# Second channel block's convolution moved from VectorE to TensorE in a gated-convolution stage, with the stage's written-out order redone

## The chip, the cores and the metric

The kernel runs on one core of a Trainium2 chip. The metric is the device time of one execution in microseconds (us). Three timed runs stand for the kernel before, and one further execution was profiled. Engines are called PE (TensorE matmul; its weight loads are listed apart as PEld), DVE (VectorE), ACT (ScalarE), POOL (GpSimd) and SP (SyncE).

## The reference

Two pre-norm layers over x of shape (8, 512, 256), float32 throughout: a selective-scan block, an attention block with a four-expert mixture, a gated-convolution block, and a second mixture. The change touches only the third, which the kernel calls stage D. Its core is:

```
xz = layernorm(x) @ W_in                       # (8,512,256) @ (256,1024)
xc, z = split(xz, 2)                           # 512 channels each
xc = causal depthwise conv, 4 taps, over the 512 positions
xc = layernorm(silu(xc), gamma, beta)
xp = xc @ W_xproj                              # 33 columns: delta, B(16), C(16)
delta = clip(softplus(xp[..., :1]))
decay = clip(exp(delta * A), 1e-6, 1)          # per position, channel and state (16)
y = xc * sum_n(B*C * decay) + xc * D
x = x + (y * silu(z)) @ W_out
```

## The kernel before, in words

The kernel is five stages, A to E, run one after the other; all five engines meet between stages. In stage D the 8 sequences are the 8 batches. The 512 channels are four blocks of 128 (c = 0 to 3, one block across the partitions), and the 512 positions are the free dimension.

**Preparing a batch.** `stats`, `rstd`, `minus` and `norm` are the layernorm; `flip` (PE, L1964) transposes it and `flipped` (ACT, L2062) evacuates it. `lift` (PE, L1974) makes one of 8 blocks of the input projection: 0 to 3 are the convolution's channels, 4 to 7 the gate z. `lifted` (ACT, L2062) evacuates it. The convolution of a block is done in one of two ways. `conv` (PE, L1982) does it as four accumulating 128x512 matmuls with a diagonal matrix for each tap, and `conved` (ACT, L2062) evacuates the result; `taps` (DVE, L2185 and L2188) does it as one tensor_scalar and three scalar_tensor_tensor. Before the change, block 0 goes through `conv` and blocks 1, 2 and 3 through `taps`. `silu` (ACT) loads an activation table, takes silu of the convolved channels (L2100), then of z (L2103), and loads the exponential's table again (L2104). `turnx` (PE, L1989) transposes 16 tiles, `stats2` (DVE, the lines L192 and L196 on PSUM), `rstd2` and `xn` (L2201) are the second layernorm, `back` (PE, L1997) transposes back, `xf` evacuates with gamma and beta, `xproj` (PE, L2006) is the 33-column projection. `pj`, `soft`, `clip`, `rep` (PE, L2015) and `scalars` (DVE, L2225 and L2227) spread delta and B*C over the partitions. `fetch` and `add` (DVE, L2167) complete the next batch's x from gathered rows.

**The units.** A batch is also 16 units; over all batches unit u runs from 0 to 127, and 4 units in turn make a group w. `grow(u)` (ACT, L2131) is an exponential over 128x2048, `scale(u)` (DVE, L2237) is four tensor_scalar that clip it and multiply by B*C, in place, in one of 10 buffers. `sum(w, q)` (PE, L2024; q = 0 to 3) sums the four units of a group over the states; q = 0 waits for `scale(4w+3)`. `wout` (ACT, L2137) evacuates the sums, `turnw` (PE, L2034) transposes them, `gate` (DVE, L2247) adds D and multiplies by silu(z)*xc, `proj` (PE, L2042) is the output projection and `acc` (DVE, L2253) adds to x.

**The order** is written out by hand, and each engine walks its own share of one list in order. At list position u the list holds `grow(u+2)`, `scale(u)`, one `sum(w, q)` with 4w+4+q = u, the steps of END at their distance from 4w+4, and one row of the plan of each batch in work. A batch x > 0 takes its plan, PLAN, one row a position, so that row k stands at position u = 16(x-1) - 10 + k; 24 rows make it overlap the plan of the next batch by 8 rows. Batch 0 takes START, which begins at position -26. PSUM products of the plan rotate through 4 banks; a product waits for the evacuation of the one four before it. The rule that sets how far ACT can run ahead is `grow(4w+10)`, which waits for `sum(w, 3)`.

These are the rows of PLAN and END that matter here, as they are before:

```
(("flipped", 0), ("flipped", 1), ("lift", 1)), (("lifted", 1), ("lift", 2)), (("taps", 1), ("lifted", 2)),
(("lift", 3),), (("lifted", 3), ("taps", 2), ("lift", 0)), (("lifted", 0), ("lift", 4)),
(("taps", 3), ("lifted", 4), ("conv", 0)), (("conved", 0), ("lift", 5)),
(("lifted", 5), ("lift", 6), ("lift", 7)), (("lifted", 6), ("lifted", 7)), (("silu",),),
END = ((4, "wout"), (5, "turnw"), (7, "gate"), (8, "proj"), (9, "acc"))
```

The first of these is row 4 of PLAN, the one with `silu` is row 14, `turnx` is row 15, `stats2` is row 16 together with the next batch's `stats` (its row 0), `xn` 17 and 18, `back` 19, `xf` and `xproj` 20, `rep` 22.

Of the kernel before, what the change touches and what calls it, by code (L numbers as in the profile page):

```python
# [25 lines left out]
class Arena:  # L26
    def __init__(self, tensor, start, end):
        self.t, self.at, self.end = tensor, start, end
# [186 lines left out]
def take_stats(ar):  # L215
    return ar.take([4, 6]), ar.take([4, 2]), ar.take([4])


class StageA:
# [89 lines left out]
    def over(self, *step):  # L309
# [29 lines left out]
        (23, ("stepped", 3), ("softh", 1), ("cliph", 1), ("duh", 1), ("fill", 0, 1), ("drive", 0, 1)), (24, ("lifted", 1), ("lifted", 2), ("lifted", 3)))  # L339
    END = (  # L340
        (3, ("recall",)), (4, ("odd",)), (8, ("back", 0)), (9, ("gate", 0), ("back", 1)),
        (10, ("gate", 1), ("back", 2), ("gate", 2), ("back", 3)), (12, ("gate", 3), ("proj", 0, 0), ("proj", 0, 1)),
        (13, ("proj", 0, 2), ("proj", 0, 3), ("proj", 0, 4)), (14, ("proj", 0, 5), ("proj", 0, 6), ("proj", 0, 7)),
        (16, ("back_to_x", 0), ("proj", 1, 0)), (17, ("proj", 1, 1), ("proj", 1, 2)),
        (18, ("proj", 1, 3), ("proj", 1, 4), ("proj", 1, 5), ("proj", 1, 6), ("proj", 1, 7)), (20, ("back_to_x", 1)))
# [3 lines left out]
    def order(self):  # L349
# [3 lines left out]
        for h in range(first - 32, 2 * K + 32):  # L353
            b, j = divmod(h, 32)
            k, f = divmod(h, 2)
            if h == self.FIRST - 32:
                out += [("tap", w) for w in range(4)] + [("tapped", w) for w in range(4)]
            pieces = [(what, y, *rest) for y in range(NB - 1) for at, *steps in self.END if at == h - 32 * (y + 1)
                      for what, *rest in steps]
# [1476 lines left out]
class StageD:  # L1836
# [6 lines left out]
    def __init__(self, m, c):  # L1843
        self.m, self.c = m, c
        ar = Arena(m.Z, m.LO, m.HI)
        self.gy = [ar.take([256]) for _ in range(4)]
        self.An = ar.take([4, 512])
        self.wout = ar.take([4, 256])
        self.win = ar.take([2, 1024])
        self.wxp = ar.take([4, 33])  # L1850
        self.rep = ar.take([4, 128])
        self.pick = ar.take([32])
        self.diag = ar.take([4, 128])
        self.dcol = ar.take([4])
        self.sb, self.sb2 = take_stats(ar), take_stats(ar)
        self.nb = ar.take([4])
        self.pj = ar.take([4, 33])
        self.src = ar.take([4, 17])
        self.dl = [ar.take([4, 4]) for _ in range(2)]
        self.bc = [ar.take([16, 4]) for _ in range(2)]  # L1860
        self.nf = ar.take([2, 512])
        self.xp = ar.take([4, 515])
        self.nt = ar.take([4, 256])
        self.xc = ar.take([4, 512])
        self.z = ar.take([4, 512])
        self.xn, self.xf = self.xp[:, :, 3:515], self.xc
        self.zx = [ar.take([4, 512]) for _ in range(2)]
        self.e = [ar.take([4, 512]) for _ in range(10)]
        self.wt = [ar.take([512]) for _ in range(2)]
        self.yf = [ar.take([4, 128]) for _ in range(2)]  # L1870
        self.wb, self.tb, self.ob = m.banks[0:2], m.banks[2], m.banks[3]
        self.steps = self.order()
        self.uses = {}
        for step in self.steps:
            if step[0] in ("flip", "lift", "conv", "turnx", "back", "xproj", "rep"):
                self.uses[step] = len(self.uses)
        self.ring = m.ring(m.banks[4:8], len(self.uses))
        self.d_gy = m.landings(0, 4, 32)
        self.s = {n: m.sem("d_" + n) for n in (
            "d_w", "d_a", "added", "pads", "an", "consts", "moments", "rstd", "nb", "nt", "prod", "conv", "gate", "xc",  # L1880
            "xn", "bc", "raw", "dl", "sc", "zx", "grow", "scale", "sum", "wt", "tw", "yf", "op", "acc")}

    def use(self, *step):
# [2 lines left out]

    PLAN = (
        (("stats",),), (("rstd",), ("minus",)), (("norm",),), (("flip", 0), ("flip", 1)),
        (("flipped", 0), ("flipped", 1), ("lift", 1)), (("lifted", 1), ("lift", 2)), (("taps", 1), ("lifted", 2)),
        (("lift", 3),), (("lifted", 3), ("taps", 2), ("lift", 0)), (("lifted", 0), ("lift", 4)),  # L1890
        (("taps", 3), ("lifted", 4), ("conv", 0)), (("conved", 0), ("lift", 5)),
        (("lifted", 5), ("lift", 6), ("lift", 7)), (("lifted", 6), ("lifted", 7)), (("silu",),),
        (("turnx", 0), ("turnx", 1), ("turnx", 2), ("turnx", 3)), (("stats2",),), (("rstd2",), ("xn", 3)),
        (("xn", 0), ("xn", 1), ("xn", 2)), (("back", 0), ("back", 1), ("back", 2), ("back", 3)),
        (("xf", 0), ("xf", 1), ("xf", 2), ("xf", 3), ("xproj",)), (("zx",), ("pj",), ("soft",)),
# [2 lines left out]

    START = (
        (("stats",), ("consts",)), (("rstd",), ("minus",), ("spread",)), (("norm",), ("decay",)), (("flip", 0), ("flip", 1)),  # L1900
        (("flipped", 0), ("flipped", 1), ("lift", 1)), (("lifted", 1), ("lift", 2)),
        (("lifted", 2), ("taps", 1), ("lift", 3)), (("lifted", 3), ("taps", 2), ("lift", 0)),
        (("lifted", 0), ("conv", 0)), (("conved", 0), ("taps", 3), ("lift", 4)), (("lifted", 4), ("lift", 5)), (("lifted", 5), ("lift", 6)),
        (("lifted", 6), ("lift", 7)), (("lifted", 7), ("silu",), ("bound",)),
        (("turnx", 0), ("turnx", 1), ("turnx", 2), ("turnx", 3)), (("stats2",),), (("rstd2",),),
        (("xn", 0), ("xn", 1), ("xn", 2), ("xn", 3)), (("back", 0), ("back", 1), ("back", 2), ("back", 3)),
        (("xf", 0), ("xf", 1), ("xf", 2), ("xf", 3), ("xproj",)), (("pj",), ("zx",), ("soft",)),
        (("clip",), ("rep",)), (("scalars",),))


    END = ((4, "wout"), (5, "turnw"), (7, "gate"), (8, "proj"), (9, "acc"))

    def order(self):
        N, out = 16 * NB, []
        for u in range(-27, N + 12):
# [6 lines left out]
            if w in range(N // 4):  # L1922
                out.append(("sum", w, j))
            for at, what in self.END:
                y = u - 4 - at
# [26 lines left out]
    def pe(self, e):  # L1952
        m, s, ring, ident = self.m, self.s, self.ring, self.m.ident
        def bank(*step):
            r = self.use(*step)
            if r >= 4:
                e.wait_ge(*ring.done(r - 4))
            return ring.buf(r)
# [18 lines left out]
        def conv(b, c):  # L1977
            e.wait_ge(s["consts"], 1)
            e.wait_ge(*ring.done(self.use("lift", b, c)))
            o = bank("conv", b, c)  # L1980
            for w in range(4):
                ins = e.matmul(o, self.diag[:, w, :], self.xp[:, c, w:w + 512], start=w == 0, stop=w == 3)  # L1982
            ins.then_inc(s["prod"], 1)

        def turnx(b, i):
# [51 lines left out]
        def proj(w):  # L2037
# [3 lines left out]
            for k in range(4):  # L2041
                ins = e.matmul(self.ob[:, 0:256], self.yf[w % 2][:, k, :], self.wout[:, k, :], start=k == 0, stop=k == 3)  # L2042
            ins.then_inc(s["op"], 1)

        self.walk(flip=flip, lift=lift, conv=conv, turnx=turnx, back=back, xproj=xproj, rep=rep, sum=sums, turnw=turnw,
                  proj=proj)

    def act(self, e):
        m, s, ring, own, vec = self.m, self.s, self.ring, self.m.own["act"], self.m.vec
# [45 lines left out]
            evac(self.xc[:, c, :], "conv", b, c)  # L2095

        def silu(b):
            e.wait_ge(*ring.done(self.use("conv", b, 0)))
            e.wait_ge(s["conv"], 3 * b + 3)
            e.activation(self.xc, self.xc, ACT.Silu).then_inc(s["xc"], 1)  # L2100
            for c in range(4, 8):
                e.wait_ge(*ring.done(self.use("lift", b, c)))
            e.activation(self.z, self.z, ACT.Silu).then_inc(s["gate"], 1)  # L2103
            e.preload_act_table_set(LN_EXP)  # L2104
# [28 lines left out]
        def wout(w):  # L2133
            e.wait_ge(s["sum"], w + 1)
            if w >= 2:
                e.wait_ge(s["tw"], w - 1)
            e.activation(self.wt[w % 2], self.wb[w % 2], ACT.Copy).then_inc(s["wt"], 1)  # L2137

        self.walk(decay=decay, rstd=rstd, norm=norm, flipped=flipped, lifted=lifted, conved=conved, silu=silu, rstd2=rstd2, xf=xf,
                  soft=soft, grow=grow, wout=wout)  # L2140

    def dve(self, e):
        m, s, ring, own, vec = self.m, self.s, self.ring, self.m.own["dve"], self.m.vec
        def consts(b):
            e.wait_ge(s["pads"], 1)
            for w in range(4):
                e.tensor_scalar(self.diag[:, w, :], m.ident, vec["conv1"][:, w:w + 1], None, ALU.mult)

        def spread(b):
            for j in range(4):  # L2150
# [100 lines left out]
        def acc(w):  # L2251
            e.wait_ge(s["op"], w + 1)
            e.tensor_tensor(m.X[:, w, :], m.X[:, w, :], self.ob[:, 0:256], ALU.add).then_inc(s["acc"], 1)  # L2253

        self.walk(consts=consts, spread=spread, bound=bound, add=add, stats=stats, minus=minus, taps=taps, stats2=stats2, xn=xn, pj=pj, clip=clip, scalars=scalars,
                  scale=scale, gate=gate, acc=acc)

# [438 lines left out]
```

## Time and profile before

| | |
|---|---|
| timed runs (3) | median 3223.49 us, 3222.7 to 3224.59 |
| profiled execution | 3224.59 us, its span 3222.8 us |
| stage D in the trace | about 2104 to 2674 us |
| mean granted TensorE clock | 0.936 of full speed |
| busy over the whole span | PE 86%, DVE 66%, ACT 50%, POOL 32% |

The stage is a sixth of the span. A row of the timeline gives the start, the time taken, the engine, the line, the shapes and, in brackets, how long the engine had been idle before it and what ended that. The profile records two matmul instructions for each float32 matmul of the code, so a `conv` of four matmuls is "x8".

### The profile page before, as it was taken

How to read it: one execution, taken by the hardware profiler on the slowest of the kernel's cores; microseconds unless marked ns; L12 is line 12 of the kernel's file. 1: busy time of each engine (PE TensorE's matmuls, PEld its weight loads, DVE VectorE, ACT ScalarE, POOL GpSimd, SP SyncE). 2: the span in 40 equal slices, each digit the busy share in tenths (PEclk: the TensorE clock that was granted, in tenths of full speed). 3: DMA queues.
4: the chain of work that ended last, by engine and by line, in shares of the span. 5: the costliest groups of instructions: out<-in, count | busy, mean ns of one | idle time of the engine just before them, and what ended most of it. 6: DMA issues, size and time to landing. Idle time of an engine off the chain costs nothing.

```text
span 3222.8 us, 40373 instructions
## 1 busy us (share of the span) xinstructions
PE 2765.5 (86%) x13718; PEld 1663.7 (52%) x13718; DVE 2132.6 (66%) x3858; ACT 1623.9 (50%) x2429; POOL 1021.4 (32%) x714
## 2 busy tenths in 40 slices
PE   7778887887765799999969999958888988999999
PEld 4445454454443455555545666634444445666666
DVE  1788888888885667777532222237777785777776
ACT  3778778877861355555441111137787781111111
POOL 0788888888881221121001000011112000100000
PEclk9899999999867899999989999978989999999999
DMA  3587887888873665555422000020000002000000
GB/s 112 120 175 148 173 174 163 148 181 169 161 176 80 191 175 95 88 93 79 68 118 80 23 23 23 15 53 11 7 7 14 1 1 59 7 14 7 7 7 14
DMA packets 119273, 262.95 MB, mean 82 GB/s; under 512 B 14784, under 2 KB 72896, under 8 KB 117408
## 3 DMA queue, kind: packets, MB, share of 16 engines
q0 software_dynamic: 24928, 134.89, 20.1%
q1 hardware_dynamic: 94144, 125.47, 16.9%
q8 instruction: 115, 1.88, 0.3%
q14 instruction: 86, 0.70, 0.1%
HBM read 135.40 MB, written 131.20 MB: 83 GB/s over the span
## 4 chain that ended last, share of the span: by engine, by line
PE 49%; issue 7%; ACT 6%; DVE 5%; DMA 1%; POOL 0%; POOLq 0%; ACTq 0%; DVEq 0%
PE PS L2401 7%; PE PS L1677 6%; PE PS L2419 6%; PE PS L1974 4%; PE PS L1699 3%; PE PS L1340 2%; ACT Z L2131 2%; PE PS L2024 2%; PE PS L1297 2%; PE PS L1319 2%; PE PS L1322 2%; PE PS L1267 2%; PE PS L2006 1%; PE PS L1272 1%; PE PS L1366 1%
## 5 line engine op out<-in xcount | busy, mean ns | idle before, releaser
L856 POOL TENSOR_TENSOR Z<-Z 128x1024 f32<-128x1024 f32 x256 | 649.4, 2764 | 123.1 <-DVE Z L757 77.4
L764 DVE TENSOR_TENSOR_SCAN Z<-PS,Z 128x1024 f32<-128x1024 f32 x256 | 576.4, 2275 | 19.6 <-ACT PS L684 10.8
L535 PE MATMUL PS<-Z 128*128 128x128 f32 x2048 | 305.4, 295 | 120.9 <-DVE Z L764 48.4
L535 PEld LDWEIGHTS PS<-Z 128*128 128x128 f32 x2048 | 250.5, 151 | 253.0 <-issue 80.1
L684 ACT ACTIVATE PS<-Z 128x511 f32<-128x511 f32 x512 | 332.7, 687 | 65.2 <-DVE Z L764 63.4
L1436 ACT ACTIVATE Z<-PS 128x512 f32<-128x512 f32 x320 | 188.9, 596 | 269.0 <-PE PS L1322 263.8
L2452 ACT ACTIVATE Z<-PS 128x512 f32<-128x512 f32 x144 | 85.9, 596 | 411.8 <-PE PS L2401 411.8
L696 ACT ACTIVATE Z<-PS,Z 128x512 f32<-128x512 f32 x378 | 245.6, 683 | 75.9 <-PE PS L535 69.3
L2401 PE MATMUL PS<-Z 128*128 128x512 f32 x576 | 273.5, 600 | 7.9 <-DVE Z L2534 7.1
L1529 DVE TENSOR_REDUCE Z<-PS 128x1 f32<-128x512 f32 (+2 forms) x384 | 182.5, 507 | 122.1 <-PE PS L1298 118.4
L2131 ACT ACTIVATE Z<-Z 128x2048 f32<-128x2048 f32 x128 | 252.6, 1999 | 14.5 <-PE PS L2024 8.8
L487 PE MATMUL PS<-Z 128*128 128x512 f32 x512 | 243.3, 604 | 10.3 <-ACT Z L604 9.5
L1677 PE MATMUL PS<-Z 128*128 x560 | 247.8, 595 | 0.6 <-issue 0.6
L2419 PE MATMUL PS<-Z 128*128 128x256 f32 x1024 | 242.9, 380 | 2.1 <-DVE Z L2549 2.1
L2419 PEld LDWEIGHTS PS<-Z 128*128 128x128 f32 x1024 | 193.6, 190 | 80.6 <-issue 53.6
L2237 DVE TENSOR_SCALAR Z<-Z 128x512 f32<-128x512 f32 x512 | 215.3, 488 | 7.5 <-ACT Z L2131 7.2
L2549 DVE SCALAR_TENSOR_TENSOR Z<-PS,Z 128x256 f32<-128x256 f32 x512 | 213.7, 475 | 9.9 <-PE PS L2419 9.9
L2534 DVE TENSOR_TENSOR Z<-Z,PS 128x512 f32<-128x512 f32 x144 | 98.2, 686 | 131.0 <-ACT Z L2452 130.6
L1804 DVE TENSOR_TENSOR Z<-Z,PS 128x512 f32<-128x512 f32 x70 | 48.1, 687 | 197.2 <-PE PS L1677 197.2
L2278 POOL TENSOR_TENSOR Z<-Z 128x512 f32<-128x512 f32 x32 | 41.5, 1327 | 428.5 <-ACT Z L2062 428.5
L2024 PE MATMUL PS<-Z 128*32 128x512 f32 x1024 | 142.0, 645 | 35.3 <-DVE Z L2237 35.3
L1677 PEld LDWEIGHTS PS<-Z 128*128 128x128 f32 x560 | 104.3, 191 | 119.2 <-issue 119.2
(297 smaller groups left out, 4930.2 us busy)
## 6 DMA issues: line engine op xcount, KB each, us to landing
sums<-Z POOLq DMA_DIRECT2D x112, 768.0 KB, 8.5
Z<-rows_b SPq DMA_DIRECT2D x128, 256.0 KB, 4.8
Z<-scr SPq DMA_DIRECT2D x256, 128.0 KB, 6.9
rows_n<-in_L_ffn_expert_wv POOLq DMA_DIRECT2D x32, 528.0 KB, 7.8
scr<-Z SPq DMA_DIRECT2D x32, 384.0 KB, 3.5
Z<-Z POOLq DMA_DIRECT2D x14, 768.0 KB, 7.5
Z<-in_L_ffn_expert_wv SPq DMA_DIRECT2D x4, 2048.0 KB, 15.1
Z<-sums SPq DMA_DIRECT2D x7, 768.0 KB, 6.3
```

The costliest lines, as they stand in the source:

```text
L487: ins = e.matmul(self.bank("conv", b, c)[0], self.conv[:, w, k, c * 128:(c + 1) * 128], self.n_fm[:, k, w:w + 512], start=i == 0, stop=i == 7)
L535: ins = e.transpose(self.turned[i % 2][:, c * 128:(c + 1) * 128], self.h(k, c // 2)[:, c % 2, i * 128:(i + 1) * 128], ident)
L684: ins = e.activation(self.aa[f][:, c, 1:512], self.de[b % 2][:, 2 * f + c, 1:512], ACT.Exp, scale=self.An[:, q:q + 1])
L696: e.activation(self.pr[k % 3][:, i - 1, :], self.turned[i % 2], ACT.Copy, scale=self.ct[b % 2][:, i, 16 + n:17 + n]).then_inc(s["yprod"], 1)
L764: e.tensor_tensor_scan(h, a, h, 0.0, ALU.mult, ALU.add).then_inc(s["scan"], 1)
L856: e.tensor_tensor(self.h(k, f), self.du[b % 2][:, 2 * f:2 * f + 2, :], b3(self.Bs[k % 2], 1, [128, 2, 512]), ALU.mult).then_inc(s["hin"], 1)
L1677: ins = e.matmul(ub[n], self.hs[c % 2][:, k, :], self.wv[:, bass.ds(expert[c] * 4096 + (2048 * k + 512 * n), 512)], start=k == 0, stop=k == 1)
L2131: e.activation(self.e[u % 10], self.An, ACT.Exp, scale=self.dl[b % 2][:, j, i:i + 1]).then_inc(s["grow"], 1)
L2237: ins = e.tensor_scalar(o, o, 1e-6, self.bc[b % 2][:, 4 * j + i, q:q + 1], ALU.max, ALU.mult)
L2401: ins = e.matmul(self.up[n % 2], w, self.nf[b % 2][:, k, :], start=k == 0, stop=k == 1)
L2419: ins = e.matmul(o[:, j * 256:(j + 1) * 256], self.hd[n % 4][:, c], self.w2[:, x - 1, :], start=True, stop=True)
L2549: ins = e.scalar_tensor_tensor(xx, o[:, j * 256:(j + 1) * 256], self.cw[b % 2][:, t, x - 1:x], xx, ALU.mult, ALU.add)
```

## The change

Block 1's convolution goes to PE as well. The diagonal matrices are built for blocks 0 and 1 (8 instead of 4 tensor_scalar at the start of the stage), `conv(1)` and `conved(1)` come into both plans and `taps(1)` goes out. The rows 4 to 14 of PLAN and the rows from 4 on of START are written anew: the lifts come in the order 2, 3, 0, 1, 4, 5, 6, 7, and `lift` 5, 6, 7 now stand together in row 13 with `lifted` 6, 7 in the row of `silu`. Row 15 on are as before, but START is two rows longer, so that `turnx` to `scalars` of batch 0 come two positions later against the plan of batch 1. In END `wout` moves from 4 to 3, `proj` from 8 to 9 and `acc` from 9 to 11.

```diff
-        self.diag = ar.take([4, 128])
+        self.diag = ar.take([2, 4, 128])
...
     PLAN = (
...
-        (("flipped", 0), ("flipped", 1), ("lift", 1)), (("lifted", 1), ("lift", 2)), (("taps", 1), ("lifted", 2)),
-        (("lift", 3),), (("lifted", 3), ("taps", 2), ("lift", 0)), (("lifted", 0), ("lift", 4)),
-        (("taps", 3), ("lifted", 4), ("conv", 0)), (("conved", 0), ("lift", 5)),
-        (("lifted", 5), ("lift", 6), ("lift", 7)), (("lifted", 6), ("lifted", 7)), (("silu",),),
+        (("flipped", 0), ("flipped", 1), ("lift", 2)), (("lifted", 2), ("lift", 3)), (("taps", 2), ("lift", 0)),
+        (("lifted", 3), ("lifted", 0), ("taps", 3), ("lift", 1)), (("lifted", 1), ("conv", 0)),
+        (("conved", 0), ("conv", 1)), (("lift", 4), ("conved", 1)), (), (("lifted", 4),),
+        (("lift", 5), ("lifted", 5), ("lift", 6), ("lift", 7)), (("lifted", 6), ("lifted", 7), ("silu",)),
...
     START = (
...
-        (("flipped", 0), ("flipped", 1), ("lift", 1)), (("lifted", 1), ("lift", 2)),
-        (("lifted", 2), ("taps", 1), ("lift", 3)), (("lifted", 3), ("taps", 2), ("lift", 0)),
-        (("lifted", 0), ("conv", 0)), (("conved", 0), ("taps", 3), ("lift", 4)), (("lifted", 4), ("lift", 5)), (("lifted", 5), ("lift", 6)),
-        (("lifted", 6), ("lift", 7)), (("lifted", 7), ("silu",), ("bound",)),
+        (("flipped", 0), ("flipped", 1), ("lift", 2)), (("lifted", 2), ("lift", 3)),
+        (("lifted", 3), ("taps", 2), ("lift", 0)), (("lifted", 0), ("taps", 3), ("lift", 1)), (("bound",),),
+        (("lifted", 1), ("conv", 0)), (("conved", 0), ("conv", 1))) + (
+        (("conved", 1), ("lift", 4)), (("lifted", 4), ("lift", 5)), (("lifted", 5), ("lift", 6)),
+        (("lifted", 6), ("lift", 7)), (("lifted", 7), ("silu",)),
...
-    END = ((4, "wout"), (5, "turnw"), (7, "gate"), (8, "proj"), (9, "acc"))
+    END = ((3, "wout"), (5, "turnw"), (7, "gate"), (9, "proj"), (11, "acc"))
...
-                ins = e.matmul(o, self.diag[:, w, :], self.xp[:, c, w:w + 512], start=w == 0, stop=w == 3)
+                ins = e.matmul(o, self.diag[:, c, w, :], self.xp[:, c, w:w + 512], start=w == 0, stop=w == 3)
...
         def silu(b):
-            e.wait_ge(*ring.done(self.use("conv", b, 0)))
-            e.wait_ge(s["conv"], 3 * b + 3)
+            for c in range(2):
+                e.wait_ge(*ring.done(self.use("conv", b, c)))
+            e.wait_ge(s["conv"], 2 * b + 2)
...
-            for w in range(4):
-                e.tensor_scalar(self.diag[:, w, :], m.ident, vec["conv1"][:, w:w + 1], None, ALU.mult)
+            for c in range(2):
+                for w in range(4):
+                    e.tensor_scalar(self.diag[:, c, w, :], m.ident, vec["conv1"][:, 4 * c + w:4 * c + w + 1], None, ALU.mult)
```

## Rows read from the trace of the kernel before

**Rows 1.** Window in stage D: length; busy PE, PEld, DVE, ACT, POOL; clock; DMA; GB/s.

```profile
2310.00:2370.00 60.00, 52.72 (x268) 25.63 (x268) 45.25 (x118) 48.09 (x47) 9.32 (x8) 0.91 0.03 10
```

**Rows 2.** Who waited for whom, 2186 to 2661 us: total, times, longest.

```profile
DVE Z L2253 <- PE PS L2042: 29.7, 12, 4.1
...
PE PS L2024 <- DVE Z L2237: 34.0, 11, 4.5
...
PE PS L1989 <- ACT Z L2100: 13.5, 7, 4.4
...
PE PS L1964 <- ACT Z L2062: 8.8, 6, 2.4
```

**Rows 3.** Timeline of PE, 2250 to 2300 us (batch 2).

```profile
2252.48 3.60 PE L1982 MATMUL PS<-Z 128*128 128x512 f32 x8
2256.01 1.06 PE L2024 MATMUL PS<-Z 128*32 128x512 f32 x8
...
2260.31 3.70 PE L1974 MATMUL PS<-Z 128*128 128x512 f32 x8
2263.94 1.92 PE L2024 MATMUL PS<-Z 128*32 128x512 f32 x16
...
2270.90 1.97 PE L1989 MATMUL PS<-Z 128*128 128x128 f32 x16 [1.52 <-ACT Z L2100]
...
2279.22 1.93 PE L2024 MATMUL PS<-Z 128*32 128x512 f32 x8 [4.50 <-DVE Z L2237]
```

**Rows 4.** Timeline of PE, the same `turnx` one batch on.

```profile
2335.91 1.97 PE L1989 MATMUL PS<-Z 128*128 128x128 f32 x16 [1.52 <-ACT Z L2100]
```

**Rows 5.** Groups by line, 2186 to 2661 us: busy us, mean ns.

```profile
L2188 DVE SCALAR_TENSOR_TENSOR Z<-Z 128x512 f32<-128x512 f32 x62 | 46.6, 752 | 2.2
...
L2185 DVE TENSOR_SCALAR Z<-Z 128x512 f32<-128x512 f32 x20 | 9.7, 485 | 10.6 <-ACT Z L2062 10.6
```

**Rows 6.** Timeline of ACT, 2262 to 2285 us.

```profile
2267.04 0.58 ACT L2137 ACTIVATE Z<-PS 128x512 f32<-128x512 f32 x1
2267.64 1.28 ACT L2100 ACT_TABLE_LOAD   x1
2268.93 1.91 ACT L2100 ACTIVATE Z<-Z 128x2048 f32<-128x2048 f32 x1
```

**Rows 7.** Timeline of DVE, 2262 to 2283 us.

```profile
2273.00 2.49 DVE L192 BATCH_NORM_STATS2 Z<-PS 128x6 f32<-128x512 f32 x4 [1.83 <-PE PS L1989]
...
2275.82 1.37 DVE L192 BATCH_NORM_STATS2 Z<-Z 128x6 f32<-128x256 f32 x4
...
2277.52 1.64 DVE L2237 TENSOR_SCALAR Z<-Z 128x512 f32<-128x512 f32 x4
```

**Rows 8.** Granted clock in two stretches of batch 2 (columns as in rows 1).

```profile
2278.00:2286.00 8.00, 6.78 (x24) 2.94 (x24) 8.00 (x20) 7.94 (x12) 0.00 (x0) 0.57 0.00 0
2295.00:2299.00 4.00, 4.00 (x13) 1.46 (x16) 2.18 (x7) 0.51 (x2) 3.09 (x4) 0.57 0.23 66
```

**Rows 9.** Timeline of PE, 2115 to 2206 us (batch 0 and the start).

```profile
2137.23 3.67 PE L1982 MATMUL PS<-Z 128*128 128x512 f32 x8 [0.73 <-issue]
...
2164.24 3.65 PE L1997 MATMUL PS<-Z 128*128 128x128 f32 x16 [9.32 <-DVE Z L2201]
2169.08 7.01 PE L2006 MATMUL PS<-Z 128*128 128x33 f32 x32 [1.19 <-ACT Z L2062]
...
2178.58 3.75 PE L1974 MATMUL PS<-Z 128*128 128x512 f32 x4 [0.73 <-issue]
```

**Rows 10.** Timeline of DVE, the start of the stage.

```profile
2119.15 0.84 DVE L2147 TENSOR_SCALAR Z<-Z 128x128 f32<-128x128 f32 x4
...
2157.88 1.40 DVE L2167 TENSOR_TENSOR Z<-Z 128x256 f32<-128x256 f32 x4
```

**Rows 11.** Timeline of ACT, first `grow` and batch 1's `silu`.

```profile
2185.86 2.00 ACT L2131 ACTIVATE Z<-Z 128x2048 f32<-128x2048 f32 x1
...
2202.62 1.28 ACT L2100 ACT_TABLE_LOAD   x1
```

## The prediction

> **What bounds the stage now.** I read four views, in this order: the busy times of a steady stretch, the list of waits, the timeline of each engine over one batch, and the granted clock of short windows.
>
> The steady stretch [rows 1] shows PE busy 52.72 of 60 us, ACT 48.09 and DVE 45.25. One batch takes 2335.91 - 2270.90 = 65.0 us, from `turnx` to the next `turnx` [rows 3, 4]. PE idles only three times in it. It waits 1.52 us for `silu` ahead of `turnx` and 4.50 us for `scale` behind it [rows 3], and some 1.3 us for `xf` (8.8 us in 6 times, the last wait of [rows 2]). So PE works 65.0 - 7.3 = 57.7 us of a batch. DVE has its own idle time, 29.7 us in all at `acc` [rows 2], and PE doesn't wait for what comes behind those. Hence in a steady batch the sum of PE's work and of its three waits is the time. A microsecond put on PE costs one, a microsecond taken from DVE gives nothing, unless it shortens one of the waits.
>
> That PE is really occupied while it is recorded as busy can be read from starts alone: `conv` starts at 2252.48 and the next matmul at 2256.01, 3.53 us for 8 instructions of 512 columns, 0.44 us each, with nothing between [rows 3].
>
> The Trainium skill, Perfetto Trace Analysis, Identifying the Most-Contended Engine, says that matmul busy time is no measure of PE's headroom and that LDWEIGHTS busy share is one, while for VectorE and ScalarE occupancy is a fair measure. By it PE (PEld 25.63 of 60) would have room, and ACT and DVE would be the contended engines. I go by the spacing of the starts, but the rule's outcome is a rival below.
>
> **The change in a steady batch (batches 2 to 7).**
>
> - *Added on PE: `conv(1)`.* 3.53 us at full clock [rows 3]. Bounds: the fall of a clock to half would make it 7.1; below 3.53 nothing in the trace suggests.
> - *Removed from DVE: `taps(1)`.* 0.485 + 3 x 0.752 = 2.74 us [rows 5]. DVE idles in each batch anyway, so 0 on the path.
> - *Added on ACT: `conved(1)`*, in place of nothing; the like evacuation is 0.58 us (`wout`, [rows 6]). ACT is idle for the whole of `conv` now, so 0.
> - *`wout` one position earlier.* It then waits for the same `sum(w, 3)` as the `grow` behind it, which it delays by 0.58 us; that `grow` is followed by the same work in sum. 0.
> - *`proj` and `acc` later.* PE's order changes (`proj` behind `sum` 1 and `turnw` instead of behind `sum` 0), its sum doesn't. The wait of `acc` for `proj`, 29.7 us of DVE, should all but go, since two positions lie between them now. Behind it on DVE stood the next batch's `add` and a `scale` which no PE wait hangs on. 0.
> - *The wait ahead of `turnx`.* It ends with `silu`, so I compare both ways from t, the start of `lift(5)` behind `sum` 3 in row 13. PE: three lifts at 3.63 / 2 (2260.31 to 2263.94) are 5.4 us. From 2263.94 to the end of `turnw` at 2270.90 - 1.52 = 2269.38 PE now does three sums, `proj` and `turnw` in 5.44 us; one of the sums (0.96, half of the 1.92) is ahead of t in the new order. So PE is at `turnx` at t + 5.4 + 4.5 = t + 9.9. ACT: `lift(7)` ends at t + 5.4, then 0.1 of latency, `lifted(7)` 0.6, table load 1.28, `silu` 1.91 [rows 6]: t + 9.3. PE comes second, the wait goes: -1.52. The margin is 0.6 us.
> - *The wait of 4.50 us behind `turnx`.* `turnx` starts at 2270.90; DVE can begin `stats2` at 2273.00, was idle for 1.83 us before it, and then runs `stats2`, the next batch's `stats` and `scale` (2277.52 + 1.64) without a gap [rows 7]. PE has two sums to do meanwhile. Every instruction of this chain and its order stay (rows 15 to 18 of the plan are untouched). `acc` now falls behind this `scale`, not in front. 4.50 us stay.
> - *Clock.* After that wait the granted clock is at half for (1 - 0.57) x 2 x 8 = 6.9 us, and again behind `xproj` for 3.4 us of a window of 4 [rows 8]. PE is idle for 0.6 us of the first, so the two cost it about 3.1 + 1.7 = 4.8 us in a batch. What stands ahead of each (4.50 us of idle time; `xproj` with its 33 columns) stays, and I take the same 4.8. The bounds are 1.7 (one short fall) and 6.8 (two long ones).
>
> The sum is 3.53 - 1.52 = +2.0 us a batch, six times +12.1. The bounds from the clock alone are 6 x (-3.1) = -19 and 6 x 2.0 = +12 around it.
>
> The Trainium skill, TensorE: Matmul & The Clock Gate, The HAM clock gate, has the clock fall after an idle stretch and come back after a busy one; the falls of this trace agree, one behind 4.50 us of idle time [rows 3, 8]. It gives no reason why a fall should go here, as the stretch of 4.50 stays.
>
> **The start of the stage and batch 1.** PE isn't the bound in it, so I follow the chain.
>
> - Four more diagonals on DVE stand between `stats` and `minus`: +0.84 [rows 10].
> - `conv(1)` of batch 0: +3.53; the 0.73 us that PE waited ahead of `conv(0)` [rows 9] goes, as `lift(1)` now lies between: together +2.8.
> - The `add` and `stats` of batch 1 stood between `stats2` and `xn` of batch 0. In the new order they come ahead of `stats2`, where DVE has nothing to do: -1.40 [rows 10] - 1.70 (2275.82 to 2277.52, [rows 7]), but the second layernorm's two small activations, hidden behind them so far, come out: +0.5. Together -2.6.
> - `flip` of batch 1 now stands ahead of `back(0)` on PE. Eight transposes are half of 3.65, 1.8 us [rows 9], half of it beside `xn`: +0.9.
> - `lift(2)` of batch 1 stands ahead of `xproj(0)`: 3.6 us at half clock (3.75 for the row at 2178.58) less the 1.19 that PE waits there now [rows 9]: +2.4.
> - From the end of `xproj` (2176.09) to the first `grow` (2185.86) lie 9.8 us [rows 9, 11]. `flip` and the gap up to 2178.58 leave it: -2.5.
> - From that `grow` to batch 1's table load are 16.8 us [rows 11], ACT without a break. ACT will have to wait for the two convolutions in it: `conv(0)` ends about 4.9 us and `conv(1)` 8.4 us after the first `grow` starts, ACT is there 0.7 and 1.1 us before: +1.8.
>
> These make +0.84 + 2.8 - 2.6 + 0.9 + 2.4 - 2.5 + 1.8 = +3.6, if the clock stays at half up to the second lift. `xproj(0)` takes 7.01 us at half clock [rows 9]; PE is busy for longer ahead of it than now, and at full clock it and a lift would save 3.5 + 1.8, which makes it -1.7. The upper bound is another lift at half clock, +5.4. I take the middle, +2.
>
> **The end of the stage.** The last batch has no successor to prepare and keeps its chain; of `proj(30)` and `turnw(31)` the order is swapped. Between -0.6 and 0; I take 0.
>
> **Sum.** 12.1 + 2.0 = +14.1 us on the profiled execution's 3224.59 (its span 3222.8), that is 3238.7. It stands 1.1 us above the median of the runs, so the predicted median is 3237.6, +0.44%. This kernel's measurement can tell about 0.2%, 6.4 us.
>
> **Rivals.**
>
> 1. *The clock falls become rarer (no measurable change).* The time that PE idles around `turnx` shrinks from 6.0 to 4.5 us, and the batch's length changes, so the falls will lie elsewhere. For it speaks that the falls follow idle time. Against it speaks that the 4.50 us stay. If each batch loses the long fall's 3.1 us or the short one's 1.7, that is 14.1 - 19 = -5 or 14.1 - 10 = +4 us: 3219 to 3228. If both go, 14.1 - 29 = -15: 3209.
> 2. *PE has room and DVE sets the pace (faster).* PE's recorded 52.72 of 60 would be partly pipelining, `conv(1)` would slip in at no cost, and DVE's 2.74 us a batch would come off: 6 x -2.74 + 2 = -14 us, 3209. It decides from the point where the matmul behind `conv(1)` starts less than 0.8 us later than without it. Against it speaks the unbroken spacing [rows 3]. It is what the skill's rule on the most-contended engine leads to.
> 3. *The wait behind `turnx` shrinks (faster).* Its place is `sum` 0 in row 18; DVE has 2.74 us less in a batch and no wait at `acc`. It decides from 2.4 us on, since then 2.0 a batch and the start are paid; all 4.50 us would make 6 x (2.0 - 4.5) + 2 = -13 us, 3210. Against it speaks that DVE was idle ahead of `stats2` [rows 7].
> 4. *The wait ahead of `turnx` stays (slower still).* The lifts 5 to 7 and `silu` stand closer together now and the margin is 0.6 us. If ACT is late by as much as now, it is 6 x 1.52 = 9 us more: 3247.
>
> **How the numbers follow.** The forecast, 3230 to 3244, has 0.52. Rival 1 has 0.17 for the part within 0.2% and 0.02 for both falls gone, rivals 2 and 3 have 0.06 and 0.04, rival 4 0.12; 0.07 is left for a new wait on PE that I don't see, slower too. Faster by over 0.2% is 0.02 + 0.06 + 0.04 = 0.12, within it 0.17, slower 0.52 + 0.12 + 0.07 = 0.71. The range leaves out the faster rivals (0.12), the lower end of rival 1 and the far end of the slower cases (0.08): 3226 to 3246.
>
> **What the profile after would show.** L1982 with 128 instructions, L2188 with 48; a batch of 67 us from `turnx` to `turnx`; the wait of L1989 for L2100 near 0 from batch 2 on; the waits of PE's L2024 for L2237 still 4.5 us each; DVE's wait of L2253 for L2042 nearly gone; batch 1's table load 2 us later than now. I am wrong if the 4.50 us shrink, if half-clock time in a batch changes by over 3 us, or if PE shows a new wait at `conv`, `rep` or `turnx`.

## The result, and the profile after

The kernel after took 3249.3 us in the median of 4 runs (3245.37 to 3251.26), the kernel before 3224.04 us (4 runs, 3222.7 to 3227.59): a ratio of 1.0076, 95% interval 1.0057 to 1.0093. Slower was forecast, but 3237.6 us with at most 3246. In the third set of experiments below the same two kernels stood at 1.0051 (1.0033 to 1.007), 3246.53 against 3229.94 us. The loss is clear of the noise both times, and its size varies.

The profiled execution of the kernel after took 3246.3 us, its span is 3244.5 us, 21.7 more than before. Windows cut both spans at the start of stage D, at the `turnx` of batch 1, at that of batch 7 and at the end of stage D. The kernel before (columns as in [rows 1]):

```profile
2103.80:2205.88 102.08, 60.03 (x185) 34.15 (x185) 46.90 (x116) 48.80 (x59) 16.51 (x17) 0.73 0.16 42
2205.88:2597.76 391.88, 347.14 (x1769) 166.12 (x1769) 296.18 (x765) 306.48 (x295) 51.40 (x44) 0.91 0.03 8
2597.76:2673.96 76.20, 63.17 (x416) 30.95 (x416) 63.98 (x165) 58.13 (x43) 5.66 (x4) 0.96 0.00 1
2673.96:3222.80 548.84, 527.16 (x1920) 350.22 (x1920) 388.28 (x937) 99.69 (x185) 48.65 (x80) 0.99 0.06 17
```

The kernel after:

```profile
2104.08:2202.62 98.54, 61.68 (x200) 33.80 (x200) 42.77 (x112) 50.55 (x61) 16.92 (x17) 0.77 0.16 44
2202.62:2614.42 411.80, 372.40 (x1817) 180.52 (x1817) 280.63 (x740) 306.47 (x301) 52.17 (x44) 0.90 0.02 7
2614.42:2690.88 76.46, 62.40 (x417) 32.22 (x416) 60.74 (x166) 58.09 (x43) 7.63 (x4) 0.93 0.00 1
2690.88:3244.50 553.62, 532.27 (x1920) 353.47 (x1920) 388.39 (x937) 99.69 (x185) 48.65 (x80) 0.97 0.05 17
```

The start of the stage became 3.5 us shorter (forecast: 2 longer). The six batches took 19.9 us more (forecast: 12.1). The end took 0.3 more. And stage E, whose instructions are the same in number, took 4.8 us more at a granted clock of 0.97 instead of 0.99. The remaining 0.3 us lie before stage D.

The timeline of PE in the kernel after, for one batch, where [rows 3] show it before (L1990 is `turnx`, L2025 `sum`, L1965 `flip`, L2007 `xproj`, L1983 `conv`):

```profile
2309.73 3.70 PE L1983 MATMUL PS<-Z 128*128 128x512 f32 x8
2313.36 1.06 PE L2025 MATMUL PS<-Z 128*32 128x512 f32 x8
2314.36 3.70 PE L1983 MATMUL PS<-Z 128*128 128x512 f32 x8
...
2326.06 5.42 PE L1975 MATMUL PS<-Z 128*128 128x512 f32 x12
...
2335.73 1.97 PE L1990 MATMUL PS<-Z 128*128 128x128 f32 x16
2337.62 1.92 PE L2025 MATMUL PS<-Z 128*32 128x512 f32 x16
2344.05 3.09 PE L2025 MATMUL PS<-Z 128*32 128x512 f32 x16 [4.50 <-DVE Z L2240]
...
2354.36 1.75 PE L1965 MATMUL PS<-Z 128*128 128x128 f32 x8 [2.06 <-ACT Z L2063]
2356.04 1.93 PE L2025 MATMUL PS<-Z 128*32 128x512 f32 x8
2357.90 3.95 PE L2007 MATMUL PS<-Z 128*128 128x33 f32 x32
2361.69 3.66 PE L1975 MATMUL PS<-Z 128*128 128x512 f32 x4
```

Two convolutions of 3.63 us and the three lifts in a row (5.42 us) stand in it, `turnx` waits for nothing, the 4.50 us behind it are unchanged. New is the wait of `flip`, 2.06 us where it was some 1.3. Behind it `flip` takes 1.75 us (8 matmuls at full clock take 1.29 elsewhere) and the `sum` 1.93 instead of 1.06; behind `xproj` the `lift` takes 3.66 instead of 1.98. These are two stretches of half clock, 1.2 instead of 2.4 GHz, with most of `xproj` at full clock between them. Two batches later they run together; from `xproj` on:

```profile
2493.58 7.04 PE L2007 MATMUL PS<-Z 128*128 128x33 f32 x32
2500.43 3.76 PE L1975 MATMUL PS<-Z 128*128 128x512 f32 x4
2504.12 1.52 PE L2025 MATMUL PS<-Z 128*32 128x512 f32 x8
```

The waits of the kernel after, 2186 to 2690 us, against [rows 2]:

```profile
PE PS L2025 <- DVE Z L2240: 34.3, 11, 4.5
...
PE PS L1965 <- ACT Z L2063: 11.7, 6, 2.1
...
DVE Z L2256 <- PE PS L2043: 4.8, 8, 0.6
...
PE PS L1990 <- ACT Z L2102: 4.8, 1, 4.8
```

DVE's wait at `acc` shrank from 29.7 to 4.8 us, PE's at `turnx` from 13.5 to 4.8 (batch 1 alone), and neither shows as a gain. PE's wait at `flip` grew from 8.8 to 11.7.

**A batch cut in two.** The reading that the experiments test comes from the starts of `turnx` and `flip` and the granted clock of the windows between them. Half-clock time is (1 - clock) x 2 x length.

| profile, batches 1 to 6 | `turnx` to `flip`, us | `flip` to next `turnx`, us | half-clock time in that second part, us |
|---|---|---|---|
| before | 18.6 in all | 46.4 46.4 46.4 46.4 46.4 48.0 | 3.7 3.7 3.7 3.7 3.7 6.7 |
| after | 18.6 in all | 46.2 49.7 49.4 49.4 52.7 52.7 | 0 7.0 6.9 6.9 13.7 13.7 |

The first part is 18.6 us in both, though its own half-clock time runs from 3.3 to 12.3 us. The second part grows with its half-clock time. At none, it is 46.2 us after; before it has 46.4 us with 3.7 of half clock in it. In the batches 2 to 4 the half-clock time of a whole batch hardly changed (10.4 us before, 10.3 after); it moved, from 6.7 and 3.7 us in the two parts to 3.3 and 7.0.

### The profile page after: what moved, and what is told of

Same layout as the page of the kernel before. It is cut to its first block, busy times and chain, and to the rows that moved or that the text cites. A ratio compares the mean times of both kernels' runs of the same rounds, so it can differ in the third digit from the quotient of the medians.

```text
span 3244.5 us, 40490 instructions
## 1 busy us (share of the span) xinstructions
PE 2797.3 (86%) x13782; PEld 1683.0 (52%) x13782; DVE 2111.5 (65%) x3830; ACT 1625.4 (50%) x2437; POOL 1024.4 (32%) x714
## 4 chain that ended last, share of the span: by engine, by line
PE 50%; ACT 7%; issue 6%; DVE 4%; DMA 1%; SPq 0%; POOL 0%; POOLq 0%; ACTq 0%; DVEq 0%
PE PS L2404 7%; PE PS L1677 6%; PE PS L2422 6%; PE PS L1975 4%; ACT Z L2133 3%; PE PS L1699 3%; PE PS L1340 2%; PE PS L2025 2%; PE PS L1297 2%; PE PS L1319 2%; PE PS L1983 2%; PE PS L1322 2%; PE PS L1267 2%; PE PS L2007 1%; PE PS L1366 1%
## 5 line engine op out<-in xcount | busy, mean ns | idle before, releaser
L764 DVE TENSOR_TENSOR_SCAN Z<-PS,Z 128x1024 f32<-128x1024 f32 x256 | 576.3, 2274 | 21.8 <-ACT PS L684 11.7
L487 PE MATMUL PS<-Z 128*128 128x512 f32 x512 | 244.2, 606 | 10.3 <-ACT Z L604 9.5
L2025 PE MATMUL PS<-Z 128*32 128x512 f32 x1024 | 146.1, 676 | 34.3 <-DVE Z L2240 34.3
```

What stands on the lines that cost most here:

```text
L487: ins = e.matmul(self.bank("conv", b, c)[0], self.conv[:, w, k, c * 128:(c + 1) * 128], self.n_fm[:, k, w:w + 512], start=i == 0, stop=i == 7)
L764: e.tensor_tensor_scan(h, a, h, 0.0, ALU.mult, ALU.add).then_inc(s["scan"], 1)
L2025: ins = e.matmul(self.wb[w % 2][32 * j:32 * j + 32, :], self.pick, self.e[(4 * w + j) % 10][:, q, :], start=q == 0, stop=q == 3)
```

## The experiments

Theory A: PE sets the second part, ACT the first, and the added convolution costs what it takes on PE. Theory B: the new order is what costs. The kernel before had medians of 3229.85, 3228.8 and 3229.94 us in the three sets (3224.04 above), with single runs from 3218.7 to 3246.7. So each kernel is judged by its ratio to the runs of the kernel before in its own set, on the same chip. The parts of a batch come from one profiled execution of each kernel.

### First set: which half of the change costs

**conv_only2.** Block 1's convolution on PE in the old rows.

```diff
-        (("flipped", 0), ("flipped", 1), ("lift", 1)), (("lifted", 1), ("lift", 2)), (("taps", 1), ("lifted", 2)),
-        (("lift", 3),), ...
+        (("flipped", 0), ("flipped", 1), ("lift", 1)), (("lifted", 1), ("lift", 2)), (("conv", 1), ("lifted", 2)),
+        (("conved", 1), ("lift", 3)), ...
```

> The convolution of block 1 on PE, but the plan's other rows and END as before the change. Theory A (what a batch costs lies on PE between flip and turnx, where the added convolution and the half-clock time count in full; the 18.6 us from turnx to flip are set by ACT): 3.6 us a batch more and the 1.5 us wait ahead of turnx partly kept, so 3240 to 3258 us, that is at least as slow as the full change (3249). Theory B (the new order itself costs time, the convolution is mostly absorbed): under 3235 us.

Measured: 1.0096 (1.0074 to 1.0118), 3261.89 us: slower than the full change, above even theory A's range in microseconds. In its profile `turnx` keeps its wait of 1.52 us from batch 2 on. The second part is 49.9 us at 3.0 us of half clock in two batches, where the kernel before has 46.4 at 3.7: +3.5. In the other four it is 51.2 to 51.5 us at 7.2.

**order_only2.** The new plans and END, block 1 on DVE.

```diff
-        (("lifted", 1), ("conv", 0)), (("conved", 0), ("conv", 1)), (("lift", 4), ("conved", 1)), ...
+        (("lifted", 1), ("taps", 1), ("conv", 0)), (("conved", 0),), (("lift", 4),), ...
```

> The new plans and the new END, but block 1 convolved by the four VectorE instructions as before. Theory A: the wait of 1.5 us ahead of turnx goes and nothing is added on PE, so 3210 to 3224 us, a batch of 62.5 to 65 us. Theory B: slower than before by 10 us or more, over 3234 us.

Measured: 0.9963 (0.9939 to 0.9987), 3219.15 us. The order is a gain, not the cost; theory B falls. Its second part is 44.1 us at 3.5 us of half clock, and 48.9 at 13.7. Three of its six batches, at 67.5 us, are longer than theory A's 65; they are those with the 13.7.

**end_only2.** The kernel before with `wout`, `proj` and `acc` moved.

```diff
-    END = ((4, "wout"), (5, "turnw"), (7, "gate"), (8, "proj"), (9, "acc"))
+    END = ((3, "wout"), (5, "turnw"), (7, "gate"), (9, "proj"), (11, "acc"))
```

> The kernel before with only wout, proj and acc moved. Theory A: the wait of acc on DVE goes, the time stays, 3219 to 3229 us. Theory B: the earlier wout or the later proj delays silu or scale by 1 us or more a batch, over 3231 us.

Measured: 1.0021 (1.0007 to 1.0034), 3238.61 us. Theory A expected nothing; it costs, and by what theory B names, a later `silu`. Its timeline of ACT ahead of `silu` (L2137 is `wout`, L2062 `lifted` 6 and 7) and the `turnx` that waits:

```profile
2336.95 0.60 ACT L2137 ACTIVATE Z<-PS 128x512 f32<-128x512 f32 x1 [3.11 <-PE PS L2024]
2337.45 1.08 ACT L2062 ACTIVATE Z<-PS 128x512 f32<-128x512 f32 x2
2338.40 2.02 ACT L2131 ACTIVATE Z<-Z 128x2048 f32<-128x2048 f32 x1
2340.44 1.28 ACT L2100 ACT_TABLE_LOAD   x1
```

```profile
2343.70 1.97 PE L1989 MATMUL PS<-Z 128*128 128x128 f32 x16 [2.77 <-ACT Z L2100]
```

`wout` now waits 3.11 us for the sums with two ready evacuations queued behind it. They are done behind the wait instead of in front, so `silu` comes later and PE waits 2.77 us instead of 1.52.

**end_back2.** The kernel after with END as before.

```diff
-    END = ((3, "wout"), (5, "turnw"), (7, "gate"), (9, "proj"), (11, "acc"))
+    END = ((4, "wout"), (5, "turnw"), (7, "gate"), (8, "proj"), (9, "acc"))
```

> The kernel after with wout, proj and acc at their old positions. Theory A: 3243 to 3255 us, as the full change. Theory B: nearer to the kernel before, under 3240 us.

Measured: 1.0025 (1.0009 to 1.0041), 3238.16 us, below theory A's range and within theory B's. In two of its three batches without half clock in the second part the two parts are 18.3 and 46.5 us, together 64.8 (65.2 in batch 1); the kernel after has 18.6 and 46.2, also 64.8. So at equal clock END is worth nothing to a batch of the new plan; it only moves 0.3 us from one part to the other. What differs in the profiles is the half-clock time in the second parts (0, 7.0, 7.0, 13.8, 0 and 0 us here, 48 us in all in the kernel after) and stage E, which is 5.0 us shorter here (below).

### Second set: is it the clock?

Theory C: at equal clock the change costs about 1.5 us a batch, the rest is half-clock time between `flip` and `turnx`. Three kernels get matmuls whose results nobody uses, 9 ahead of the `sum` that waits behind `turnx` and 8 ahead of `flip` from batch 2 on, so that PE isn't idle there. They write a PSUM bank that is free at that time.

```diff
+        def fill(o, n):
+            for _ in range(n):
+                e.matmul(o[:, 0:256], self.win[:, 0, 0:128], self.wout[:, 0, :], start=True, stop=True)
...
+            if b > 1 and kb == 0:
+                fill(self.wb[0], 8)
             e.wait_ge(s["nt"], b + 1)
...
+                if w % 4 == 1 and w < 28:
+                    fill(self.wb[w % 2], 9)
                 e.wait_ge(s["scale"], 4 * w + 4)
```

**fill_before**, the filling in the kernel before:

> The kernel before with idle PE filled: 9 extra matmuls of 128x256 (3.9 us at full clock) ahead of the sum that waits 4.5 us behind turnx, and 8 (3.5 us) ahead of flip, from batch 2 on; their results are not used. Theory C (the changed kernel's batches are longer by 1.6 us at equal clock, and the rest of the loss is half-clock time that falls between flip and turnx): the first clock fall goes, turnx to flip stays 18.6 us, flip to turnx is 44.7 to 46.4 us; 3205 to 3225 us by the ratio, 0.995 to 1.000. Rival D (the clock is a mere companion): the extra 7.4 us a batch show in part, over 1.005.

**fill_after**, in the kernel after:

> The same filling in the kernel after. Theory C: half-clock time between flip and turnx falls from 7 and 14 us a batch to under 3.5, that stretch is 46.2 to 48 us in every batch, and the time comes within 0.5% of the filled kernel before: ratio to the kernel before 0.997 to 1.003. Rival D: it stays at 1.007 or above.

**fill_order**, in the new plans with block 1 on DVE and END as before:

> The new plans with block 1 convolved on DVE as before, END as before, and the filling. Theory C: flip to turnx is 42.5 us at full clock, 2.1 us a batch under the kernel before and 3.7 under the kernel after; ratio to the kernel before 0.988 to 0.995, the fastest of the three filled kernels. Rival D: not faster than the filled kernel before.

Measured: 1.0003 (0.9993 to 1.0013), 1.0033 (1.002 to 1.0046) and 0.9922 (0.9906 to 0.9937). The timeline of PE in fill_after (L1963 the filling, L1971 `flip`, L1996 `turnx`):

```profile
2334.55 4.15 PE L1963 MATMUL PS<-Z 128*128 128x256 f32 x18
2339.13 1.92 PE L2033 MATMUL PS<-Z 128*32 128x512 f32 x16 [0.42 <-DVE Z L2248]
...
2347.20 3.62 PE L1963 MATMUL PS<-Z 128*128 128x256 f32 x16
2350.66 1.04 PE L1971 MATMUL PS<-Z 128*128 128x128 f32 x8
...
2352.62 3.76 PE L2013 MATMUL PS<-Z 128*128 128x33 f32 x32
2356.21 1.96 PE L1981 MATMUL PS<-Z 128*128 128x512 f32 x4
...
2396.60 1.93 PE L1996 MATMUL PS<-Z 128*128 128x128 f32 x16
```

The 7.04 us of `xproj` and the slow `lift` behind it are gone. The batches at full clock:

| at no half clock | `turnx` to `flip` | `flip` to `turnx` |
|---|---|---|
| fill_before | 19.4 | 44.47 |
| fill_after | 19.9 | 45.94 |
| fill_order | 19.2 | 42.51 |

In the second part the order saves 44.47 - 42.51 = 1.96 us, and the change as a whole costs 45.94 - 44.47 = 1.47. The difference of fill_after and fill_order, 3.43, is not the convolution's price, since they differ in END too, and END moves 0.3 us out of the second part. The pair that differs in the convolution alone is end_back2 and order_endold (third set), both with END as before. At no half clock their second parts are 46.54 and 42.76 us, their first parts 18.27 in both: the convolution costs 3.78 us a batch. PE's timeline, here of end_back2, shows where it goes:

```profile
2585.78 1.07 PE L2025 MATMUL PS<-Z 128*32 128x512 f32 x8
2586.78 3.70 PE L1983 MATMUL PS<-Z 128*128 128x512 f32 x8
2590.41 1.07 PE L2025 MATMUL PS<-Z 128*32 128x512 f32 x8
2591.41 1.99 PE L2043 MATMUL PS<-Z 128*128 128x256 f32 x8
```

and order_endold, without it:

```profile
2447.91 1.92 PE L2025 MATMUL PS<-Z 128*32 128x512 f32 x16
2449.76 1.99 PE L2043 MATMUL PS<-Z 128*128 128x256 f32 x8
```

From start to start the convolution takes 3.63 us. The two `sum` that it parts take 1.00 us each instead of 1.85 together, 0.15 more. The other rows of the two batches are alike.

The first two time expectations were missed by a little (1.0003 for at most 1.000, 1.0033 for at most 1.003), since the filling is too long: it runs over into `flip`, which no longer waits, and makes the first part 0.6 to 1.3 us longer, in every second batch of fill_after even 2.9. PE sets the first part there, and half clock is no longer free in it: with 3.4 us of it fill_after has 21.5 us instead of 19.86, 0.48 us for each us. The distance of the two filled kernels is 0.3%, that of the unfilled ones 0.76% in the first comparison and 0.51% in the third set. D falls: extra work of 7.4 us a batch costs the kernel before nothing measurable.

**norm_pool.** The kernel after, with the four activations of `norm` on GpSimd for batches 1 to 7.

```diff
+        def norm(b):
+            if not b:
+                return
...
+            for i in range(4):
+                ins = e.tensor_scalar(self.nt[:, i, :], m.X[:, 4 * b + i, :], r[:, i:i + 1], self.nb[:, i:i + 1], ALU.mult,
+                                      ALU.add)
+            ins.then_inc(s["nt"], 1)
```

> The kernel after with the four normalizing activations of batches 1 to 7 moved from ACT to GpSimd. Theory C with its second part (the stretch from turnx to flip is set by ACT's list, whatever PE's clock): the stretch shortens by up to the 2.0 us that leave ACT, to 16.6 to 17.3 us, the wait at flip shrinks from 2.1 to under 1 us. Rival E (PE or DVE sets the stretch): it stays at 18.6 us or grows because GpSimd is slower than ACT at it.

Measured: 0.9965 (0.9951 to 0.9979), faster than before although the convolution is still on PE. `turnx` to `flip` is 16.63 us in five of the six batches, 2.0 less, and `flip` waits no more:

```profile
2286.66 3.11 POOL L2292 TENSOR_SCALAR Z<-Z 128x256 f32<-128x256 f32 x4 [46.14 <-DVE Z L2179]
```

```profile
2290.64 1.94 PE L1998 MATMUL PS<-Z 128*128 128x128 f32 x16 [0.57 <-issue]
2292.55 1.29 PE L1965 MATMUL PS<-Z 128*128 128x128 f32 x8
```

ACT's list set the first part: it gave back what was taken from ACT, and PE's half-clock time in it (3.3 or 7.0 us) made no difference. The second part gained as well: with no wait at `flip`, and nothing filled in, its half-clock time is 3.8 us in five batches and 0 in one, 19 us in all where the kernel after has 48.

### Third set: the change again, and what is better

**after_again.** The kernel after, unchanged.

> The changed kernel once more, on the chip of the three kernels beside it. Theory C (1.5 us a batch and the rest is half-clock time that scatters from execution to execution): ratio to the kernel before 1.003 to 1.009, single runs apart by 10 us or more. Rival: the loss of 25 us is fixed, ratio 1.007 to 1.009 and runs within 6 us.

Measured: 1.0051 (1.0033 to 1.007), runs from 3242.01 to 3255.47 us. The scatter is as expected, but the profile repeats: its six batches are 64.83, 68.31, 68.06, 68.02, 71.28 and 71.35 us, those of the first profile of this kernel 64.84, 68.27, 68.04, 68.02, 71.28 and 71.35.

**order_endold.** The new plans, block 1 on DVE, END as before (order_only2 with END as in end_back2).

> The new plans with block 1 on DVE as before and END as before: of the change only the order of the rows. Theory C: 2.0 us a batch less than before at equal clock, ratio 0.990 to 0.998. Rival (the gain of the other kernels of this order came from the filling or from GpSimd): 0.999 or above.

Measured: 0.9953 (0.9935 to 0.9972), 3217.01 us. Its six second parts give the price of the clock within one kernel: 42.8 us at no half clock, 44.5 at 3.6, 46.0 at 6.4, 49.3 at 13.8, that is 0.47 to 0.51 us for each us. At no half clock a batch is 18.27 + 42.76 = 61.0 us; the kernel before, less 0.47 x 3.7, is at 63.3. So the order saves 2.3 us a batch and the convolution costs 3.8, which leaves the 1.5 of the whole change.

**norm_pool_order.** That with `norm` on GpSimd.

> The same, with the normalizing activations of batches 1 to 7 on GpSimd. Theory C: turnx to flip 16.6 us and flip to turnx 42.5 to 46 us, so 4 us a batch less than before, ratio 0.984 to 0.992. Rival (DVE or ACT sets a batch once PE has this much room): no better than the kernel without it.

**fill_norm_order.** That with the 9 matmuls ahead of `sum` and none ahead of `flip`.

> The same again, with the 9 filling matmuls ahead of the sum behind turnx and none ahead of flip. Theory C: the clock fall behind that wait goes, the stretch of 16.6 us keeps its length as it isn't set by PE, half-clock time between flip and turnx doesn't grow; ratio 0.980 to 0.990. Rival: the filling only costs, ratio above that of the unfilled kernel.

Measured: 0.9869 (0.9846 to 0.9892), 3189.91 us, and 0.9863 (0.9839 to 0.9886), 3190.19 us. The batches are 59.1 to 60.8 us in both. The filling removes the first fall (no half-clock time between `turnx` and `flip` from batch 2 on), which costs nothing there, and leaves the one behind `xproj` (3.6 us in three of six batches in either). So it brings nothing measurable, as the second part of theory C says, and the unfilled kernel is the one to keep: 1.3% faster than before, 1.8% faster than the change. `norm` on GpSimd lowers the half-clock time of the six second parts here too, from 33.8 us in order_endold to 10.8.

## Why the prediction was wrong, point by point

Direction and main mechanism were right: PE had no room, and DVE's 2.74 us and its 29.7 us of waiting were worth nothing. The size was off, 25 us for 14. In the profiled executions it is 21.7 for 14.1: the six batches took 7.8 us more than forecast and stage E 4.8, the start 5.5 less. By steps:

- *`conv(1)` at 3.53 us*: 3.63 by the starts in the new order, and 3.78 with the two `sum` that it parts. Nearly right.
- *`taps(1)` at 0, the wait of 4.50 us stays*: right, 4.50 in each of the batches 2 to 6.
- *The wait ahead of `turnx` goes, margin 0.6 us*: right, no `turnx` waits from batch 2 on. Rival 4 didn't happen.
- *The sum of +2.0 a batch at equal clock*: 1.5. The convolution costs 0.25 more than forecast, the order saves 2.3 us where I had only the 1.52 ahead of `turnx`; where the other 0.7 come from was not taken apart.
- *"I take the same 4.8"*, the clock term: this is the step that failed. It had two faults. I priced both falls by their length, 3.1 for the one behind the 4.50 us and 1.7 for the one behind `xproj`; but the first lies in the stretch that ACT sets, and costs nothing. And I let the second be as before. It was 25.2 us of half-clock time in the six second parts before and 48.3 after, 23 us more, which at 0.47 make 10.9 us. Six times 1.5 and these 10.9 make 19.9, what the batches grew. In the batches 2 to 4 the half-clock time was the same in sum, as I had assumed; 3.3 us of it had moved from the part where it is free to the part where it costs. The trace of before had the warning: the first part was 18.63 to 18.65 us in every batch although its half-clock time was 10.1 in one and 6.7 in the others. I added PE's waits up over a whole batch and didn't ask what set each part of it. My own sign of being wrong, half-clock time in a batch changing by over 3 us, came in the batches 5 and 6 (20.4 us for 10.4 and 13.4). My upper bound for the clock, +12 us, would have reached 3250, and the range stopped short of it. Rival 1 had the falls move, but to become rarer.
- *The waits of PE are three and their sum is fixed but for `turnx`*: the one of `flip` grew from 1.3 to 2.06 us in most batches, since PE comes to it sooner (its `proj` takes 1.95 us ahead of it instead of 3.78 at half clock) and ACT doesn't. By itself this costs nothing, as the first part stays at 18.6 us; what follows it is the half clock of the second part.
- *END at 0*: 0 for a batch of the new plan at equal clock, +1.0 us a batch on the old one, where the wait of `wout` keeps two ready evacuations waiting. I had said that the earlier `wout` delays only the `grow` behind it; I had not looked at the row of `lifted` between.
- *The start, +2 (bounds -1.7 and +5.4)*: -3.5, outside the bounds. The clock came up ahead of `xproj(0)`, as the timeline of PE in the kernel after shows; it took 3.65 us where [rows 9] have 7.01. That is the case that I had at -1.7. The rest is the last term: from the first `grow` to the table load of batch 1 are 17.2 us (2182.17 to 2199.37), 0.4 more than before, where I had put 1.8 for waits on the two convolutions.

```profile
2170.39 1.99 PE L1975 MATMUL PS<-Z 128*128 128x512 f32 x4
2172.21 3.65 PE L2007 MATMUL PS<-Z 128*128 128x33 f32 x32
2175.70 3.68 PE L1975 MATMUL PS<-Z 128*128 128x512 f32 x8
```

- *Stage E at 0*: +4.8 us at 0.97 instead of 0.99 of the clock. The profiles have stage E at two lengths, counted from the matmul behind PE's first wait in it, of 4.5 us, to the end of the span: 543.0 to 544.9 us, or 547.4 to 549.8. All six profiles with the new END have the longer one, those without the added convolution too; of the eight with the old END seven have the shorter one, conv_only2 among them, and order_endold the longer. So it goes with END but for one profile, and not with the convolution. How END reaches into stage E was not looked into.

Rival 2, with the rule of the Trainium skill, Perfetto Trace Analysis, Identifying the Most-Contended Engine, would have made 3209 us. Its share of LDWEIGHTS, 43% of the stretch, is no headroom here: the 3.63 us of matmuls that were put into it cost 3.78 us.

Shown are the cost of the convolution, the gain of the order, ACT's hold on the first part and the price of half clock in the second. That the half-clock time there grows with the wait of `flip` is made likely: with `norm` on GpSimd the wait goes, and the half-clock time falls from 48 to 19 us in the one pair and from 34 to 11 in the other; the filling in fill_after takes away both as well. In the eight profiles with `norm` on ACT and nothing filled, the ten second parts with 13.6 to 13.8 us all stand behind a wait of 1.96 to 2.07 us. But the wait doesn't settle it: waits of 2.04 to 2.39 us are also followed by 3.7 to 7.2 us, and fill_before, where `flip` doesn't wait, has 3.7 us in three second parts and 6.7 in one. Why the pattern of the six batches repeats from one execution to another is open too, and so is how much of end_back2's lead over the full change is its pattern.

## What to carry to other kernels

Cut the repeating unit where one engine's waits end, and ask of each part what sets its length: the same wait or slow clock is free in the one part and costs in full in the other. Where two engines are both near their limit, moving work from the second to the first costs all of it; look for the instructions that stand in the list of the engine that sets a part, and for an engine that is idle: four small operations taken from ACT to GpSimd were worth 2 us a batch at equal clock, about as much as the whole reordering (2.3), and 0.8% of the time against its 0.5%. When a `wait` moves ahead in a hand-written order, read what is queued behind it on its engine, also the steps that the edit doesn't name.

## What the runs showed of the hardware

- Half clock has a price by place: none in 18.6 us with 3.3 to 12.3 us of it, 0.47 to 0.51 us for each us in the second part of order_endold, where PE sets the pace. In fill_after, where PE sets the first part too, it costs 0.48 there.
- The clock fell to half while PE was recorded busy without a break: behind `xproj`, 32 instructions of 33 columns, the `lift` took 3.6 us instead of 1.96 in batch 2 of the kernel before. In the kernel after `xproj` took 3.76 us in batch 1 and 7.04 us in batch 5, where the clock was at half when it began and stayed there through it and the `lift` behind it.
- The lengths of six batches, with their clock falls, were the same to 0.04 us in two profiled executions of the kernel after, while single runs of one kernel scattered by 25 us (3222.12 to 3246.7 us for the kernel before in one set).
- Four scaled copies of 128x256 took 3.11 us on GpSimd, and 2.06 us on ACT.
